# Mixture-of-experts kernel: which tiles start before the routing is known, and when the tile table is made

## The reference

```python
h = tokenizer(x)                       # 128 sequences x 124 patches, 256 features: linear, layer norm
h = h + attention(layernorm(h))        # inside each sequence of 124
f = layernorm(h)
p = softmax(relu(f @ rw1 + rb1) @ rw2 + rb2)      # six experts
top_w, top_i = top_k(p, 2)
g = softmax(top_w)
e = relu(relu(f @ w1[e] + b1[e]) @ w2[e] + b2[e]) @ w3[e] + b3[e]   # 256 -> 256 -> 256 -> 256
h = h + sum over the two chosen experts of g * e
```

## Time and profile before

| what | value |
|---|---|
| median of 3 runs | 1242.8 us (1240.68 to 1245.06) |
| the profiled execution | 1239.83 us, its span 1238.0 us |
| busy: PE, DVE, ACT, POOL | 1182.6, 977.5, 819.2, 880.0 us |
| granted clock of PE, mean | 0.988 |
| data moved by DMA | 195.49 MB, mean 158 GB/s |

### The profile page before, as it was taken

The page is one execution under the profiler, slowest core; times in us unless marked ns, Lnnn a source line. Parts: engine busy times, 40 slices in busy tenths (PEclk is TensorE's granted clock), DMA queues, the critical chain, the costliest instruction groups (busy, mean ns, idle before and its releaser), DMA issues.

```text
span 1238.0 us, 27898 instructions
## 1 busy us (share of the span) xinstructions
PE 1182.6 (96%) x7784; PEld 1050.3 (85%) x7784; DVE 977.5 (79%) x3290; ACT 819.2 (66%) x1967; POOL 880.0 (71%) x674
## 2 busy tenths in 40 slices
PE   6999999999999999999889999999999999999994
PEld 5888988898889888988678888989988888899983
DVE  5678888888888888887688786788877787788773
ACT  4788888888888888886445554645655655555542
POOL 2227888888888788887788675766775786677566
PEclk9999999999999999999899999999999999999997
DMA  3324655454445445654589979877888788887865
GB/s 121 123 91 125 161 149 151 122 134 127 126 122 136 126 127 140 175 161 125 131 191 279 238 135 273 174 141 148 175 214 208 149 172 197 214 164 165 223 122 60
DMA packets 146470, 195.49 MB, mean 158 GB/s; under 512 B 38920, under 2 KB 104204, under 8 KB 146316
## 3 DMA queue, kind: packets, MB, share of 16 engines
q1 hardware_dynamic: 71036, 125.04, 32.9%
q0 software_dynamic: 74016, 67.88, 32.7%
q10 hardware_dynamic: 1264, 0.79, 0.2%
HBM read 162.79 MB, written 99.09 MB: 212 GB/s over the span
## 4 chain that ended last, share of the span: by engine, by line
PE 62%; SPq 10%; issue 8%; ACT 7%; DVE 5%; POOL 4%; DMA 3%; POOLq 0%; ACTq 0%; DVEq 0%
PE bank L961 18%; PE bank L752 16%; PE bank L989 9%; SPq L496 6%; PE bank L906 4%; PE bank L807 3%; PE bank L892 3%; POOL expert_rows L666 3%; PE bank L950 3%; DMA half_sb<-split_weights 2%; PE bank L798 2%; PE bank L852 2%; PE bank L914 1%; SPq L503 1%; ACT rec L1056 1%
## 5 line engine op out<-in xcount | busy, mean ns | idle before, releaser
L735 POOL DMA_INDIRECT out<-yo,tail x236 | 378.1, 1602 | 133.7 <-issue 73.3
L666 POOL DMA_INDIRECT expert_rows<-rec,row_i x256 | 355.0, 1387 | 78.0 <-issue 67.0
L1172 ACT ACTIVATE h2v<-bank,small 128x512 f32<-128x512 f32 x118 | 81.3, 690 | 226.4 <-PE bank L961 205.6
L989 PE MATMUL bank<-w_sb,h_hi 128*128 128x256 f32 x944 | 186.4, 290 | 3.3 <-issue 3.3
L961 PE MATMUL bank<-h_hi,w_sb 128*128 128x512 f32 x472 | 157.0, 393 | 3.9 <-issue 3.6
L961 PE MATMUL bank<-x_hi,w_sb 128*128 128x512 f32 x472 | 157.0, 394 | 3.5 <-DVE x_lo L1613 2.9
L989 PEld LDWEIGHTS bank<-w_sb,h_hi 128*128 128x128 f32 x944 | 153.0, 194 | 4.0 <-issue 3.9
L989 PE MATMUL bank<-w_sb,h_lo 128*128 128x256 f32 x472 | 134.6, 285 | 0.0
L752 PE MATMUL bank<-tok_proj,xT_hi 128*124 128x256 f32 x512 | 101.1, 290 | 9.0 <-DVE tok_proj L1198 9.0
L961 PEld LDWEIGHTS bank<-h_hi,w_sb 128*128 128x128 f32 x472 | 88.8, 188 | 23.4 <-issue 5.5
L961 PEld LDWEIGHTS bank<-x_hi,w_sb 128*128 128x128 f32 x472 | 89.4, 189 | 22.5 <-issue 3.1
(11 more groups left out here) (243 smaller groups left out, 3104.7 us busy)
## 6 DMA issues: line engine op xcount, KB each, us to landing
w_sb<-split_weights SPq DMA_DIRECT2D x165, 512.0 KB
xg<-expert_rows SPq DMA_DIRECT2D x59, 530.0 KB
half_sb<-split_weights SPq DMA_DIRECT2D x33, 512.0 KB
out<-h SPq DMA_DIRECT2D x32, 496.0 KB
split_weights<-half_w SPq DMA_DIRECT2D x36, 256.0 KB
x_in<-in_x SPq DMA_DIRECT2D x32, 250.0 KB
small<-in_esmall SPq DMA_DIRECT2D x59, 134.0 KB
raw_w<-in_eweights SPq DMA_DIRECT2D x36, 128.0 KB
```

What stands on the lines that cost most here:

```text
L666: pool.indirect_dma_start(rows_dram, bass.IndirectOffsetOnAxis(ap=row_i[0:TOK, slot, j, k:k + 1], axis=0), rec[0:TOK, slot, j, :], None).t ...
L735: pool.indirect_dma_start(out, bass.IndirectOffsetOnAxis(ap=kept_tail(t)[:, j, E8:].bitcast(I32), axis=0), sums_out(t)[:, j, :], None, com ...
L989: mm = pe.matmul(banks[6 + b][:, i * D:(i + 1) * D], act[:, c, j * P:(j + 1) * P], w[:, 2, c, wh, :], start=(c == 0 and p == 0), stop=(c = ...
L1172: act.activation(h2v[:, m, 0:cols], banks[bank + m][:, 0:cols], ACT.Relu, bias=small_in(t)[:, DC + m:DC + m + 1]).then_inc(S["h2_v"], 1)
```

## The change

`EARLY` goes from 6 to 8: the first eight tiles are of the expert chosen early. `DECIDE` goes from 19 to 24 with it, since by then the fullest expert must have eight full tiles. Rows and weights of tiles 0 to 3 are issued in steps 29 to 32 of the pipeline instead of 26 to 31. Behind the pipeline the biases of tile 4 come first, then the six pads in pairs behind the rows of tiles 6 and 7 and behind the biases of tile 5, and the table is written, read back and waited for in SP's turn for t = 4. DVE makes the two tables in seven portions, behind tiles 2 to 8, instead of three behind tiles 2 to 4.

```diff
--- before.py
+++ after.py
@@ -56,8 +56,8 @@
 REC = D + E8 + 1
 SLOTS = 4
 WSLOTS = 2
-EARLY = 6
-DECIDE = 19
+EARLY = 8
+DECIDE = 24
 NCHUNK = NE * 3 * DC
 FIRST_CHUNKS = 4
 assert 3 * FIRST_CHUNKS + G - 2 * FIRST_CHUNKS == NCHUNK
@@ -447,12 +447,16 @@
                     sp.wait_ge(S["pool_const"], 21)
                 if DEPTH <= it < DEPTH + 2 + SPARE:
                     spare_rows(it - DEPTH)
-                if DRAIN - 7 <= it < DRAIN - 5:
-                    early_rows(it - (DRAIN - 7))
-                if DRAIN - 5 <= it < DRAIN - 5 + WSLOTS:
-                    early_weights(it - (DRAIN - 5))
-                if DRAIN - 3 <= it < DRAIN - 1:
-                    early_rows(it - (DRAIN - 3) + 2)
+                if it == DRAIN - 4:
+                    early_weights(0)
+                if it == DRAIN - 3:
+                    early_rows(0)
+                    early_rows(1)
+                if it == DRAIN - 2:
+                    early_weights(1)
+                    early_rows(2)
+                if it == DRAIN - 1:
+                    early_rows(3)
 
             def early_expert():
                 sp.wait_ge(S["early"], 5)
@@ -570,37 +574,46 @@
                     if since == 3:
                         half_layers(k, (1, 2))
 
-            for t in range(SLOTS, EARLY):
+            for t in range(SLOTS, SLOTS + 2):
                 next_rows(t)
+            wait_apart(sp, S["y_dve"], (BIG[0].q + 1) * 4, S["sp_passed"])
+            load_small(SLOTS)
             sp.wait_ge(S["table"], PADS_AT)
-            for e in range(NE):
+
+            def write_pads(e):
                 at = sp.value_load(pad_at[0:1, e:e + 1], min_val=0, max_val=NE * REGION)
                 sp.dma_start(rows_dram[bass.ds(at, TILE), :].rearrange("(p j) n -> p (j n)", p=P),
                              pad_rows[:].rearrange("p j n -> p (j n)")).then_inc(S["pads_written"], 16)
-            for t in range(SLOTS, EARLY):
-                wait_apart(sp, S["y_dve"], (BIG[t - SLOTS].q + 1) * 4, S["sp_passed"])
-                load_small(t)
-            sp.wait_ge(S["table"], TABLE_AT)
-            sp.dma_start(tab_dram, t_coli[0:NT, :]).then_inc(S["tab_kept"], 16)
-            sp.wait_ge(S["tab_kept"], 16)
-            sp.dma_start(tab[:], tab_dram.rearrange("(o t) k -> o (t k)", o=1)).then_inc(S["tab_loaded"], 16)
-            sp.wait_ge(S["tab_loaded"], 16)
-            for i in range(SENT):
-                sp.wait_ge(scattered[i], sent_to(i, G))
-            sp.wait_ge(S["pads_written"], 16 * NE)
-            next_rows(EARLY)
+
+            def load_table():
+                sp.wait_ge(S["table"], TABLE_AT)
+                sp.dma_start(tab_dram, t_coli[0:NT, :]).then_inc(S["tab_kept"], 16)
+                sp.wait_ge(S["tab_kept"], 16)
+                sp.dma_start(tab[:], tab_dram.rearrange("(o t) k -> o (t k)", o=1)).then_inc(S["tab_loaded"], 16)
+                sp.wait_ge(S["tab_loaded"], 16)
+                for i in range(SENT):
+                    sp.wait_ge(scattered[i], sent_to(i, G))
+                sp.wait_ge(S["pads_written"], 16 * NE)
 
             for t in range(1, NT):
                 q, behind = BIG[t].q, BIG[t - 1].q
                 if EARLY <= t + WSLOTS < NT:
                     wait_apart(sp, S["h1_ps"], (q + 1) * 2, S["sp_passed"])
                     load_layers(t + WSLOTS, (0,))
-                if t + SLOTS + 1 > EARLY:
+                if t + SLOTS + 1 < EARLY:
+                    next_rows(t + SLOTS + 1)
+                if t < SLOTS:
+                    for e in range(2 * t - 2, min(2 * t, NE)):
+                        write_pads(e)
+                if t + SLOTS == EARLY:
+                    load_table()
+                    next_rows(EARLY)
+                if t + SLOTS >= EARLY:
                     next_rows(t + SLOTS + 1)
                 if EARLY <= t + 1 < NT:
                     wait_apart(sp, S["y_ps"], (behind + 1) * 2, S["sp_passed"])
                     load_layers(t + 1, (2,))
-                if EARLY <= t + SLOTS - 1 < NT:
+                if SLOTS < t + SLOTS - 1 < NT:
                     wait_apart(sp, S["y_dve"], (behind + 1) * 4, S["sp_passed"])
                     load_small(t + SLOTS - 1)
                 if EARLY <= t + WSLOTS < NT:
...
@@ -1662,9 +1691,17 @@
                 if t.q == 2:
                     tile_table_rows()
                 if t.q == 3:
+                    tile_table_ends()
+                if t.q == 4:
                     tile_table_experts()
-                if t.q == 4:
+                if t.q == 5:
+                    tile_table_order()
+                if t.q == 6:
                     half_table()
+                if t.q == 7:
+                    half_table_experts()
+                if t.q == 8:
+                    half_table_waits()
             rows_out(ORDER[-1])
```

More of the change, by code:

```diff
@@ L1511, in tile_table_rows, with tile_table_ends @@
                 v.tensor_copy(t_nt[R, :], t_ti[R, :]).then_inc(s, 1)
+            def tile_table_ends():
+                s = S["table"]
                 v.wait_ge(s, 5)
@@ L1538, in tile_table_experts, with tile_table_order @@
                                 t_exp[R, 0:1].to_broadcast([TOK, 2]), ALU.not_equal).then_inc(s, 1)
+            def tile_table_order():
+                s = S["table"]
                 v.tensor_tensor(t_seq[R, :], t_exp[R, 0:2], t_ge[R, 0:2, NE - 1], ALU.add).then_inc(s, 1)
@@ L1565, in half_table, with half_table_experts @@
                 v.tensor_tensor(u_pairs[R, :], u_pairs[R, :], t_early[R, :], ALU.add).then_inc(s, 1)
+            def half_table_experts():
+                s = S["halves"]
                 v.wait_ge(s, 7)
@@ L1587, in half_table, with half_table_waits @@
                 v.tensor_reduce(u_row[R, :], u_step[R, 0:NE], AX_X, ALU.add).then_inc(s, 1)
+            def half_table_waits():
+                s = S["halves"]
                 v.wait_ge(s, 17)
```

## The result

| | median, us | range | runs |
|---|---|---|---|
| before | 1243.9 | 1240.7 to 1245.6 | 4 |
| after | 1263.7 | 1260.9 to 1266.2 | 4 |

Ratio after to before 1.017, interval 1.0141 to 1.0198: some 20 us slower, where 1241.2 and "no change" had been forecast, and far outside the range given. The profiled execution after took 1264.93 us, its span 1263.1 us, 25.1 us more than the span before.

The account below looks back on a forecast made before the run. PE's waits were taken to set the end, SP's queue, never waiting from 649.54 to 750.47 us, to limit the gain: +0.7 - 1.6 - 0.7 = -1.6 us, median 1242.8 to 1241.2; own range 1238.5 to 1244.5, all cases 1235.8 to 1247.2.

Parts of the forecast that it names:

- First rows: Before tile 0's turns near 552 us: rows land by about 555.1, a PE gap of 2.9 us, q_proj 1.5 us later.
- d: PE's delay from tile 0's late rows, 1.5 us plus 1.7 of clock: 3.2 us, from 1.5, at most 6.2.
- The clock step: Behind the gap before tile 0's turns, PE's clock granted at 0.83 over ten microseconds: 1.7 us lost, or nothing.
- the prediction's own sign: In the profile after, no PE gap at 552 us, or one over 5 us, would show the first-rows step wrong.
- Biases, tiles 6 and 7: PE's gaps for tile 4's biases, tile 6's rows and weights, and the half table go: 5.35 us gained.
- The table: Tile table ready only behind the split of tile 5's second layer; its write and read-back take 4.7 us, before 7.7.
- T' = 664.1 + d: Time in us when SP has the table: made at 659.4 + d, plus a round trip of 4.7 us.
- d - 2.5: How much later SP reaches a given command behind the table: +0.7 us with d = 3.2, -1.0 with 1.5.
- First half tile: half_sb lands in 4.2 us instead of 5.84 as weight loads leave its place: -1.6 us; fifth half tile -0.7.
- Rival 4: POOL decides: its additions begin at 641.4 whatever PE does, an earlier PE would only wait: 1242.8 us, chance 0.06.
- The prediction's first premise: PE works 96% of the span, so the end moves only with PE's waits and the order loads reach it.
- Rival 3: Tile 0's rows hold up PE in step 31, d = 6.2: 1248.0 us, chance 0.12; decides once d passes 4.7.

Follow-up runs that it names:

- experiment 9: Kernel before, with the half tiles' rows added into a scratch tensor and POOL's waits around them left out: 1239.7 us, ratio 0.9991.
- experiment 10: Changed kernel with choice at group 19, first loads at their old place, half tiles' rows in a scratch tensor without POOL's waits around them: 1240.1 us, ratio 0.9994.
- experiment 1: Changed kernel, with rows and biases of tile 0 issued in step 30 ahead of the store of h: 1256.9 us, ratio 1.0094.
- experiment 4: Changed kernel, with the half tiles' rows added into a scratch tensor and POOL's hold and follow waits left out: 1248.2 us, ratio 1.0052.
- experiment 5: Kernel before, six first tiles, with the choice at group 24 and first loads in steps 29 to 32: 1253.5 us, ratio 1.0092.
- experiment 3: Changed kernel, eight first tiles, with the expert chosen at group 19 and first loads where they were before: 1253.2 us, ratio 1.008.
- experiment 6: Kernel before, with the half tiles behind tiles 12, 16, ..., 52 instead of 14, 18, ..., 54: 1261.1 us, ratio 1.0166.
- experiment 13: Kernel before, with POOL waiting ahead of tiles 17 and 33 until the tile in front has landed: 1246.1 us, ratio 1.0044.

## Why the prediction was wrong, step by step

- **First rows (the step that failed first).** The term d was taken as 3.2 us. Measured by tile 0's first layer, 579.08 us against 568.43 before, it was 10.65. The load took 10.79 us in the chain, not 3.5. The step from the fall of the core's traffic to "so that load has landed by about 555.1" was the error: in the trace after the traffic falls too (188 and 147 GB/s in the two microseconds from 554), and the load was still on its way. Traffic carries no names. The trace before holds the answer, though no view prints it: of tile 2's rows, the load issued at 551.58 that served as the measure, 11 of 16 semaphore updates are recorded, seven of them by 555.15 and the last at 562.07, 10.5 us after the issue. It stood behind the same store of h. The upper bound from half_sb, 6.58 us, was short as well, since no such store stood ahead of that one. The clock step held: the granted clock is 0.50, the lower level of 1.2 GHz, while PE takes up work again. The turns began at 562.20; with the forecast's 1.65 us behind them d would be 8.5, so some 2.1 us are the clock's, against 1.7 forecast. By the prediction's own sign, a gap of over 5 us at 552, the first step is wrong.

```profile
555.00:560.00 5.00, 0.00 (x0) 0.00 (x0) 3.85 (x16) 1.38 (x9) 4.27 (x5) 0.63 0.68 211
560.00:565.00 5.00, 2.80 (x14) 2.83 (x15) 0.00 (x0) 0.00 (x0) 4.15 (x4) 0.50 0.48 140
...
579.08 0.48 PE L974 MATMUL bank<-x_hi,w_sb 128*128 128x512 f32 x1
```

- **Biases, tiles 6 and 7.** The gaps at 647 and 662 are gone as forecast. The 1.21 us of tile 6's rows came back as 1.05 at tile 8.
- **The table.** Right. The round trip took 4.9 us, 4.7 forecast, and with d = 10.65 the formula T' = 664.1 + d gives 674.75; the first register load is at 674.30. Tile 12's rows left SP 8.2 us later; the formula d - 2.5 says 8.15. The 7.7 us before weren't the table's alone: in the chain before, SP goes on to the table when POOL's last scatter has landed, at 648.06.

```profile
639.78 8.28 DMA expert_rows<-rec,row_i
```

In the chain after:

```profile
669.39 2.83 DMA tile_table<-t_coli
...
672.24 1.89 DMA tab<-tile_table
...
674.30 0.44 SPq L500
...
683.70 2.95 issue
686.65 8.60 PE bank L974 x24
```

- The last two rows are the gap before tile 7's second layer: 1.8 forecast, 2.95 found.
- **First half tile.** half_sb landed in 4.80 us against 5.84: 1.0 of relief, 1.6 forecast. PE's own lag behind before fell by more than forecast: by 4.5 us over the first half tile and by 1.3 over the fifth, forecast 1.6 and 0.7. With the measured d the prediction's sum for PE is 8.15 - 1.6 - 0.7 = 5.85 us late; PE's last product is 4.2 us late. So the account of SP and PE was right in kind. With the rows in time (experiments 9 and 10) PE's last product starts 1.3 us earlier.
- **Rival 4, "POOL decides" (the step that failed worst).** It was named, at 0.06, with a price of nothing, as if POOL could only withhold a gain. The prediction's first premise, that "the end moves only with what PE waits for", fell with it: PE's last product moved by 4.2 us and the end by 25.1. The page gave POOL 71% and so it looked idle. But POOL's time is additions plus landings, and the landings are not in its busy time: in a round they take it from 33.8 to 40.3 of 41.7 us. The prediction even named the switches that move, to 17 and 33, and used them for the weight loads only. It never asked what POOL does at a switch.
- **Rival 3** had the right place and sign for the first half of the loss, at 0.12 and 1248.0; d passed its point of 4.7 by far. The late rows by themselves came to 7 to 12 us, by experiments 1, 4 against 10, and 5.
- **What stays open.** Experiments 3, 6 and 9 against 10 place the second half of the loss at POOL's waits around half tiles and switches, and experiment 13 gives the two moved switches half of it. What lengthens the other landings isn't shown.

## What to carry to other kernels

An engine that waits for its own transfers is as full as its busy time plus those waits: work out its round before calling it idle, and look where its waits coincide, since moving one piece of a schedule can turn one shared wait into two. Take a landing time only from a transfer that something waited for, and with the same queue in front of it; a fall of the traffic proves nothing. When a wait is shifted into a queue with less than its length of slack, the cost can exceed the wait: here some 10 us for the eight first tiles, of which the two waits alone made 5. And before a trace is read for the size of an effect, see where its execution lies among the others: experiment 3's was 8 us above its median.

## What was not expected of the hardware

- A load of 530 KB issued 3.9 us behind a store of 496 KB on the same queue took 10.79 us; tile 8's, in the tile phase, 4.49. In experiment 1, issued at 542.13 ahead of the store, its last recorded update comes 7.6 us later. The waits are for the last of 16 parts; 12 had landed after 4.2 us.
- The waits for the indirect additions differ from kernel to kernel: the 22 around half tiles averaged 3.8 us before and 4.5 in the changed kernel, and one took 8.2 in experiment 1.
- The kernel with choice at 19 spreads from 1247.8 to 1263.2 us over nine runs, 15 us, where the kernel before, beside it, spreads over 10 in 23. Experiment 5, whose POOL keeps the phase, spreads over 4.6 in its four. That the phase in which landings meet loads isn't the same in each execution would explain it; no run shows it.
